# Four stacked graph layers on one core: inputs laid out transposed on the host, small chains merged, new PSUM homes and load order

## The reference

```python
# layer 0: Xp = x Wp + bp (8 heads of 32); out = relu(tanh(adj * (Xp C^T) Xp^T) Xp)
# layer 1: two hypergraph convolutions D^-1 H B^-1 H^T (x W^T) + b with H = (adj != 0);
#          between them relu and a LayerNorm with gamma and beta; result y + x
# layer 2: e = leaky_relu(s_j + s_i + ab), T = adj*exp(e) / row sum;
#          relu( x Wk0 + T x Wk1 + T T x Wk2 + biases )
# layer 3: xg = x * sigmoid(deg Wd + bd); qk = sigmoid(xg Wqk^T + bqk);
#          S = (qk qk^T) * adj / row sum; relu( S xg Wl^T + bl + xg Wr^T )
x = layernorm(x + L0(x, adj)); x = layernorm(x + L1(x, adj))
x = layernorm(x + L2(x, adj)); x = layernorm(x + L3(x, adj))
```

## Time and profile before

| | before |
|---|---|
| median of 3 runs | 2132.2 us (2131.32 to 2135.13) |
| span of the profiled execution | 2128.7 us |
| busy: PE, PE weight loads | 1964.9 us (92%), 1659.1 us (78%) |
| busy: VectorE, ScalarE, GpSimd | 1660.7 us (78%), 1271.3 us (60%), 862.6 us (41%) |
| DMA | 97.20 MB, 46 GB/s on average |
| share of the chain that ended last | PE 45%, DVE 25%, issue 14%, ACT 10%, POOL 5% |

### The profile page before, as it was taken

One profiled execution on the slowest core, in us unless ns is written; L12 is line 12 of the kernel. 1 busy time (PEld: TensorE's weight loads), 2 busy tenths in 40 slices (PEclk: granted clock), 3 DMA queues, 4 the chain that ended last, 5 costly groups with the idle time before them and its releaser, 6 DMA issues.

```text
span 2128.7 us, 52096 instructions
## 1 busy us (share of the span) xinstructions
PE 1964.9 (92%) x15270; PEld 1659.1 (78%) x15270; DVE 1660.7 (78%) x4520; ACT 1271.3 (60%) x2508; POOL 862.6 (41%) x1677
## 2 busy tenths in 40 slices
...
DMA packets 106517, 97.20 MB, mean 46 GB/s; under 512 B 12928, under 2 KB 97664, under 8 KB 106496
## 3 DMA queue, kind: packets, MB, share of 16 engines
...
...
## 4 chain that ended last, share of the span: by engine, by line
PE 45%; DVE 25%; issue 14%; ACT 10%; POOL 5%; DVEq 1%; SPq 0%; ACTq 0%; DMA 0%; POOLq 0%
PE psum L983 27%; DVE stats L669 5%; PE psum L1162 3%; PE psum L996 3%; PE psum L1105 3%; PE psum L1113 3%; ACT z L600 3%; PE psum L1034 2%; DVE res L882 2%; DVE hid L704 2%; DVE hid_stats L802 2%; POOL hid_rstd L422 2%; DVE xT_lo L662 2%; ACT hid_relu L507 2%; ACT e_neg L584 2%
## 5 line engine op out<-in xcount | busy, mean ns | idle before, releaser
L413 POOL TENSOR_TENSOR xg_lo<-xg,xg_hi 128x512 fp32r<-128x512 f32 x64 | 82.5, 1289 | 649.1 <-ACT xg_hi L463 649.1
L481 ACT ACTIVATE x<-res,shift,rstd 128x256 f32<-128x256 f32 x512 | 280.2, 600 | 13.6 <-POOL shift L395 12.2
L463 ACT ACTIVATE xT_hi<-psum 128x512 fp32r<-128x512 f32 x128 | 76.7, 599 | 306.7 <-PE psum L996 306.7
L669 DVE BATCH_NORM_STATS2 stats<-res 128x6 f32<-128x256 f32 x512 | 192.8, 419 | 8.9
L983 PE MATMUL psum<-wk_hi,xT_hi 128*128 128x258 f32 (+1 forms) x512 | 192.8, 377 | 1.1 <-DVE xT_lo L662 1.1
L388 POOL TENSOR_TENSOR var_eps<-mean_var,eps 128x2 f32<-128x2 f32 x256 | 50.6, 198 | 349.9 <-DVE mean_var L678 349.9
L392 POOL TENSOR_TENSOR rstd<-var_eps,minus_half 128x2 f32<-128x2 f32 x256 | 179.3, 700 | 20.0
L600 ACT ACTIVATE z<-hid_relu,hid_bias,hid_rstd 128x512 f32<-128x512 f32 x128 | 97.5, 809 | 137.9 <-POOL hid_bias L425 137.9
L983 PE MATMUL psum<-wk_hi,xT_lo 128*128 128x258 f32 (+1 forms) x512 | 174.2, 340 | 0.0
L983 PE MATMUL psum<-wk_lo,xT_hi 128*128 128x258 f32 (+1 forms) x512 | 173.8, 340 | 0.0
L689 DVE TENSOR_TENSOR masked<-psum,adjT 128x512 f32<-128x512 f32 x256 | 158.4, 682 | 6.9 <-PE psum L1013 6.9
...
## 6 DMA issues: line engine op xcount, KB each, us to landing
x_in<-in_x SPq DMA_DIRECT2D x64, 256.0 KB, 2.8
x<-x_in SPq DMA_DIRECT2D x64, 256.0 KB, 2.3
adjT<-adjT SPq DMA_DIRECT2D x128, 128.0 KB, 2.0
out<-x SPq DMA_DIRECT2D x64, 256.0 KB, 2.2
...
wk_f<-in_L_gnn_Wk SPq DMA_DIRECT2D x3, 256.0 KB, 6.1
```

Of the source, the lines that this page charges most:

```text
L413: pool.tensor_tensor(xg_lo[:, :, :, :], xg[:, :, :, :], value(xg_hi[:, :, :, :]), ALU.subtract) \
L463: return act.activation(dst, src, ACT.Copy).then_inc(sem(name), 1)
L481: last = act.activation(xs[k + 1][:, g, :], res[k][:, g, :], ACT.Identity, scale=rstd[k][:, g:g + 1], bias=shift[k][:, g:g + 1])
L669: last = dve.bn_stats(stats[k][:, g, :], res[k][:, g, :])
```

## The change

1. The host lays the inputs out: `xt` (x transposed) and `adj_t` (adj transposed) beside x, each weight group in one array (`w0` to `w3`) and each group of vectors in one (`v0` to `v3`). The transposes of x, adj and the weights on TensorE go, with their evictions. adj_t is loaded from HBM four times, once for each stage that needs it, in place of the copies inside SBUF; x is loaded to `x0` from HBM.
2. `xT0_hi` is made by ScalarE from SBUF, and `xT0_lo` by GpSimd as the first operation of its turn, in place of VectorE.
3. VectorE: the last column of `inc_b` by `tensor_tensor` (times one) in place of `tensor_copy`; sums and reciprocals of both graphs of `mix` and of `hop1` in one operation each; `node_r` without `deg_p`.
4. GpSimd: `qk + 1` by `tensor_scalar`; `x1_rest` in one add, as layer 1 is computed at half size (W2, beta and b2 halved, eps quartered).
5. Waits are put so that the one for this turn's data comes last. Every tenant has a new bank. SyncE's turn has a new order and a sixth stage, which holds only the store.
6. The weights' preparation is spread out: `prepare_0` ahead of turn 0, the others ahead of turns 0 to 3, engine by engine.

```diff
+    ("rz_0", 4, 4, "rz_read_0"), ("rz_1", 0, 4, "rz_read_1"), ("xp", 3, 0, "xp_read"),
+    ("mix_0", 5, 4, "mix_read_0"), ("xT2", 7, 2, "xT2_lo"), ("prop", 6, 1, "prop_read"), ("xpT", 2, 0, "xpT_read"),
+    ("mix_1", 4, 4, "mix_read_1"), ("deg", 0, 3, "gate"), ("y0_0", 3, 2, "y0_read_0"), ("y0_1", 7, 2, "y0_read_1"),
+    ("pxT", 5, 1, "pxT_lo"), ("xcT", 6, 0, "xcT_read"), ("y12_0", 2, 2, "y12_read_0"),
+    ("hid_0", 5, 1, "hid_read_0"), ("si", 0, 2, "e_both"), ("xT3", 4, 3, "xg"), ("hid_1", 1, 1, "hid_read_1"),
+    ("y12_1", 2, 2, "y12_read_1"), ("att_0", 0, 0, "masked_0"), ("att_1", 1, 0, "masked_1"),
+    ("att_2", 4, 0, "masked_2"), ("att_3", 7, 0, "masked_3"), ("hop1_0", 5, 2, "hop1_read_0"),
+    ("hop1_1", 6, 2, "hop1_read_1"), ("hop2", 6, 2, "hop2_read"), ("zT_0", 1, 1, "zT_lo_0"),
+    ("zT_1", 0, 1, "zT_lo_1"), ("qkT", 4, 3, "qk_tanh"), ("y1_0", 1, 1, "y1_read_0"), ("y1_1", 0, 1, "y1_read_1"),
+    ("headsT", 3, 0, "headsT_read"), ("gram", 2, 3, "scores"), ("conv", 1, 1, "res1"), ("heads", 5, 0, "res0"),
...
+                if on[1]:
+                    await_on_sp("masked_3", p[1])
+                    sp.dma_start(adjT[0][:, :, :].rearrange("p g n -> p (g n)"),
+                                 rows_at(adj_t, (t.i - 1) * (G * P * P))).then_inc(sem("adj0_loaded"), 16)
+                    await_on_sp("res0", p[1])
+                    sp.dma_start(xs[0][:, :, :], pair_at(x, (t.i - 1) * (G * P * D))).then_inc(sem("x0_loaded"), 16)
                 if on[4]:
-                    await_on_sp("x4", n[4])
-                    sp.dma_start(pair_at(out, (t.i - 4) * (G * P * D)), xs[4][:, :, :]).then_inc(sem("stored"), 16)
+                    await_on_sp("scores", p[4])
+                    await_on_sp("deg", p[4])
+                    sp.dma_start(adjT[3][:, :, :].rearrange("p g n -> p (g n)"),
+                                 rows_at(adj_t, (t.i - 4) * (G * P * P))).then_inc(sem("adj3_loaded"), 16)
+                if on[3]:
+                    await_on_sp("alpha", p[3])
+                    sp.dma_start(adjT[2][:, :, :].rearrange("p g n -> p (g n)"),
+                                 rows_at(adj_t, (t.i - 3) * (G * P * P))).then_inc(sem("adj2_loaded"), 16)
+                if on[5]:
+                    await_on_sp("x4", n[5])
+                    sp.dma_start(pair_at(out, (t.i - 5) * (G * P * D)), xs[4][:, :, :]).then_inc(sem("stored"), 16)
+                if on[0]:
+                    await_on_sp("xT0_hi", p[0])
+                    await_on_sp("xT0_lo", p[0])
+                    sp.dma_start(xt_in[:, :, :, :].rearrange("p c g n -> p (c g n)"),
+                                 rows_at(xt, t.i * (G * P * D))).then_inc(sem("xt_loaded"), 16)
+                    await_on_sp("inc", p[0])
+                    await_on_sp("edge_w", p[0])
+                    sp.dma_start(adjT[1][:, :, :].rearrange("p g n -> p (g n)"),
+                                 rows_at(adj_t, t.i * (G * P * P))).then_inc(sem("adj1_loaded"), 16)
+
+            def prepare_0():
+                sp.dma_start(wts0[:, :], w0).then_inc(sem("w_0"), 16)
+                sp.dma_start(vec0[:, :], v0.partition_broadcast(P)).then_inc(sem("w_0"), 16)
+
+            def prepare_1():
+                sp.dma_start(wts1[:, :], w1).then_inc(sem("w_1"), 16)
+                sp.dma_start(vec1[:, :], v1.partition_broadcast(P)).then_inc(sem("w_1"), 16)
+                sp.dma_start(wts2[:, :], w2).then_inc(sem("w_2"), 16)
+                sp.dma_start(vec2[:, :], v2.partition_broadcast(P)).then_inc(sem("w_2"), 16)
+                sp.dma_start(wts3[:, :], w3).then_inc(sem("w_3"), 16)
+                sp.dma_start(vec3[:, :], v3.partition_broadcast(P)).then_inc(sem("w_3"), 16)
+
+            turns(sp, turn, [(0, prepare_0), (1, prepare_1)])
...
+                if on[0]:
+                    wait(pool, "xp", p[0])
+                    wait(pool, "xT0_hi", n[0])
+                    pool.tensor_tensor(xT0_lo[:, :, :, :], xt_in[:, :, :, :], value(xT0_hi[:, :, :, :]), ALU.subtract) \
+                        .then_inc(sem("xT0_lo"), 1)
...
                     wait(pool, "x1", n[1])
-                    wait(pool, "res1", p[1])
-                    pool.tensor_tensor(x1_rest[:, :, :], xs[1][:, :, :], xs[1][:, :, :], ALU.add) \
-                        .then_inc(sem("x1_twice"), 1)
-                    wait(pool, "x1_twice", n[1])
-                    pool.tensor_tensor(x1_rest[:, :, :], x1_rest[:, :, :], rows(b2_bc), ALU.add) \
+                    pool.tensor_tensor(x1_rest[:, :, :], xs[1][:, :, :], rows(b2_half), ALU.add) \
                         .then_inc(sem("x1_rest"), 1)
                 if on[4]:
-                    rstd_of(3, t)
-                if on[3]:
-
+                    rstd_of(3, n[4], p[4])
+                if on[3]:
                     wait(pool, "qk_tanh", n[3])
-                    pool.tensor_tensor(qk[:, :, :, :].rearrange("p c g n -> p (c g) n"),
-                                       qk[:, :, :, :].rearrange("p c g n -> p (c g) n"),
-                                       ones[:, :].unsqueeze(1).to_broadcast([P, NC * G, P]), ALU.add) \
+                    pool.sem_inc(sem("pool_waits"), 1)
+                    pool.tensor_scalar(qk[:, :, :, :], qk[:, :, :, :], 1.0, 1.0, ALU.add, ALU.mult) \
                         .then_inc(sem("qk"), 1)
                 if on[2]:
-                    rstd_of(2, t)
-                if on[1]:
-                    rstd_of(1, t)
+                    rstd_of(2, n[2], p[2])
+                if on[1]:
+                    rstd_of(1, n[1], p[1])
...
-                    act.activation(adjT[0][:, :, :].rearrange("p g n -> p (g n)"), ps("adjT")[:, 0:G * P],
-                                   ACT.Copy).then_inc(sem("adjT_read"), 1)
+                    wait(act, "xt_loaded", n[0], 16)
+                    hi(xT0_hi[:, :, :, :], xt_in[:, :, :, :], "xT0_hi")
...
+            def prepare_0():
+                act.wait_ge(sem("w_0"), 32)
+                act.activation(wp_hi[:, :, :], wp_f[:, :, :], ACT.Copy).then_inc(sem("w_hi"), 1)
+
+            def prepare_1():
+                act.wait_ge(sem("w_1"), 32)
+                act.activation(w1_hi[:, :, :], w1_f[:, :, :], ACT.Copy).then_inc(sem("w_hi"), 1)
+                act.mul(b2_half[:, :], b2_bc[:, :], 0.5).then_inc(sem("b2_half"), 1)
+                act.mul(gamma_h[:, :], gamma_c[:, :], 0.5).then_inc(sem("halves_1"), 1)
+                act.wait_ge(sem("halves_1"), 1)
+                for k in range(NK):
+                    last = act.activation(w2_f[:, k, :], w2_raw[:, k, :], ACT.Copy, scale=gamma_h[:, k:k + 1])
+                last.then_inc(sem("w2_f"), 1)
+                act.wait_ge(sem("w2_f"), 1)
+                act.activation(w2_hi[:, :, :], w2_f[:, :, :], ACT.Copy).then_inc(sem("w_hi"), 1)
+
...
+            turns(act, turn, [(0, prepare_0), (0, prepare_1), (1, prepare_2), (1, prepare_3), (3, prepare_4)])
...
-                if on[0]:
-                    wait(dve, "xT0_hi", n[0])
-                    wait(dve, "xp", p[0])
-                    lo(xT0_lo[:, :, :, :].rearrange("p c g n -> p (c g n)"), ps("xT0"),
-                       value(xT0_hi[:, :, :, :]).rearrange("p c g n -> p (c g n)"), "xT0_lo")
...
+                    wait(dve, "mix_1", n[4])
+                    sums, _ = both("mix_0", "mix_1", slice(D, D + 1))
+                    dve.tensor_scalar(att_s[:, :].unsqueeze(2), sums, 1e-6, None, ALU.add).then_inc(sem("attn_0"), 1)
+                    wait(dve, "attn_0", n[4])
+                    dve.reciprocal(att_r[:, :], att_s[:, :]).then_inc(sem("attn_1"), 1)
+                    wait(dve, "res3", p[4])
+                    wait(dve, "r_bias", n[4])
+                    wait(dve, "attn_1", n[4])
+                    _, in_order = both("mix_0", "mix_1", slice(D, D + 1))
...
+                    dve.tensor_scalar(inc[:, :, :], adjT[1][:, :, :], 0.0, None, ALU.not_equal).then_inc(sem("inc"), 1)
+                    wait(dve, "prop", p[0])
+                    wait(dve, "adj1_loaded", n[0], 16)
+                    dve.tensor_tensor(inc_b[:, :, P:P + 1], adjT[1][:, :, 0:1], ones[:, 0:G].unsqueeze(2), ALU.mult) \
+                        .then_inc(sem("edge_w"), 1)
                     wait(dve, "inc", n[0])
...
+            def prepare_1():
+                dve.wait_ge(sem("w_1"), 32)
+                dve.wait_ge(sem("consts"), 1)
+                for k in range(NK):
+                    last = dve.tensor_scalar(beta_bc[:, k, :], ones[:, :], beta_c[:, k:k + 1], 0.5, ALU.mult, ALU.mult)
+                last.then_inc(sem("beta_bc"), 1)
+                dve.wait_ge(sem("w_hi"), 2)
+                lo(w1_lo[:, :, :], w1_f[:, :, :], value(w1_hi[:, :, :]), "w_lo")
+                dve.wait_ge(sem("w_hi"), 3)
+                lo(w2_lo[:, :, :], w2_f[:, :, :], value(w2_hi[:, :, :]), "w_lo")
+                dve.wait_ge(sem("beta_turned"), 1)
+                dve.tensor_copy(beta_w2[:, :], ps("conv")[:, 0:D]).then_inc(sem("beta_w2"), 1)
...
```

(19 more changed lines are left out.)

987 lines of the change are left out of this document (456 added, 531 removed), and 5 rows, old and new, of the table TENANTS.

## The result

| kernel | median us | runs | against the kernel before, 95% interval | profiled span us | mean granted clock |
|---|---|---|---|---|---|
| before, beside it | 2133.28 | 4 | 1 | 2128.7 | 0.986 |
| after | 2279.58 | 4 (2278.72 to 2284.47) | 1.0698 [1.0681, 1.0715] | 2276.9 | 0.952 |

The change makes the kernel 7.0% slower. The forecast was 2159 us with 2118 to 2200: the sign was right, the size was not, and the range does not hold the time.

The account below looks back on a forecast made before the run. A turn's period, on a chain through all engines, was taken as the bound: 1.51 - 0.5 - 0.45 = +0.56 us over 62 turns, +35, start -8, giving 2155.7; with 3.5 for the median 2159 us, range 2118 to 2200.

Parts of the forecast that it names:

- The mechanism: Turn's close: `xT0_lo` on GpSimd queues behind `rstd_of(1)`, so `xp` moves away from the variance of `res1` by +1.51 us.
- The variance to `xp`: From the end of `res1`'s variance to the start of `xp`: 2.82 us where it was 1.31, +1.51 us a turn.
- the last rival: TensorE before `xp`: idling about 2 us halves its clock for a while; no size of its own; chance 0.02.
- The term of the handovers: At `xT2_hi`, `xT2_lo` and `alpha`, putting the late wait last saves 0.45 us a turn, at most 0.46.
- What VectorE gives back: VectorE beside GpSimd's `qk`: a shorter hold lets the variance of `res1` come 0.5 us earlier, at most 0.74.
- the rival "not held": VectorE's new operation beside `qk` is not held: +0.32 us a turn, 2144 us; chance 0.22.
- One of the rivals' times: TensorE's removed work counts in full, 0.57 + 0.45 us a turn: 2065 us; chance within the 0.17.
- Start and end: Before and after the looped turns: spread-out preparation gains 8 us at the start, between 2 and 13; the end 0.
- Costed at nothing: SyncE's `xt` load behind the store, adj loads, new PSUM banks, `x1_rest` and `deg_p`: 0, banks at worst 0.1 us.

Follow-up runs that it names:

- the kernel with fillers: The kernel after, with fourteen products that nothing needs put on TensorE ahead of the wait for `xT0_lo`: 2206.23 us, 1.0352 of the kernel before.
- the mends: Kernel after with `xT0_lo` ahead of `rstd_of(1)`: 2107.57 us; also ahead of `rstd_of(2)`, `xt` load before store: 2091.28; five wait pairs restored: 2070.84; layer 3 adj load first: 2056.9.

## Why the prediction was right and wrong

- **The mechanism held.** `xT0_lo` behind `rstd_of(1)`, TensorE idle 1.5 to 2.5 us before `xp`, released by GpSimd, `res1` 0.1 to 0.4 behind `conv`: each is in the trace. The variance to `xp` was to take 2.82 us and takes 3.04: `var_eps` comes 0.07 later, by the order of its two waits, and 0.18 of issue stand ahead of `xT0_lo`, where I had put nothing.
- **The step that failed is the last rival.** "TensorE's longer idle stretch (about 2 us before `xp`) halves its clock for a while", chance 0.02, counted with the slow cases at no price of its own. It happens in 48 of 59 turns and costs 73 us, half of the loss. The evidence against it was one row, a `gram` behind 2.27 us of idling, and it couldn't bear that. The reading of the row was right: `gram` covers 1.16 us, in the kernel after the falls come 0.0 to 1.1 us behind the start of `xp`, and the clock stays up behind the row too. But one event says little where the clock spares every fifth or sixth turn: the kernel after keeps it in 11 of 59. Windows of the kernel before, behind that `gram`:

```profile
2096.00:2097.00 1.00, 1.00 (x10) 0.96 (x10) 0.06 (x1) 0.00 (x0) 0.84 (x2) 1.00 0.67 228
2097.00:2098.00 1.00, 1.00 (x6) 0.83 (x5) 0.37 (x1) 0.00 (x0) 0.06 (x1) 1.00 0.10 34
```

  A forecast that makes TensorE idle where it never did should have priced the half clock, from the work behind the stretch: some 3 us at half speed are 1.5 us a turn, 90 us over 60. That case gives 2249 us, and with a fair chance the range would have reached there.
- **The term of the handovers was mis-sized.** Forecast -0.45 us a turn; the trace has +0.21 from `xp` to `conv`. At the three places the gain is 0.23 us against the kernel before, half of what was taken: the gaps fell to 0.10 to 0.13 and not to 0.03 to 0.07. Five other handovers lost 0.33 us by the same rewriting, 0.26 of it between `xp` and `conv`. I had read their 0.03 to 0.07 us as "handovers with one late wait", and they were handovers with the late wait first and one behind it: I compared durations, not the order of the waits in the code. Some 0.2 us of the 0.44 isn't found in these. The relu and `e_exp` keep part of it (0.08 and 0.03 us with their order put back, 0.03 and 0 in the kernel before); the rest stays open.
- **What VectorE gives back** was 0.5 and is 0.65 at the start of `res1`, 0.69 by its variance. The argument was right in part: a two-input product is held, as I assumed, by `qk` for as long as it lasts. But in nearly every turn of the kernel after the product starts 0.05 us ahead of `qk` and takes 0.155 us; that it escapes is luck of the order. `qk` takes 0.62 us, near my lower bound of 0.58 and under the 0.8 that I took. So the rival "not held" described the turn, by a reason that is wrong.
- **The sum without the clock**: -0.69, +1.73 and +0.21 make +1.25 us a turn, where I had -0.5, +1.51 and -0.45, +0.56 in all. Over 62 turns that puts the forecast's sum at about 2202 us; the kernel with fillers measured 2206, just over the top of the range. Of the 121 us by which the forecast is short, 47 are what that kernel takes more than the forecast, most of it the handovers (0.66 us a turn, 41 us), and 73 are the clock. One of the rivals' times was added up wrongly: 0.57 + 0.45 a turn and the start's 8 give 2061 us and not 2065; nothing rests on it.
- **Start and end.** `xp` of the third pair starts at 81.84 us instead of 89.19: 7.4 us earlier, forecast 8. The first starts at 17.5 us (forecast 19 to 20). By the fifth pair the loss of the partly filled turns has taken 6.5 of it again.
- **Costed at nothing**: SyncE's load of `xt` was hidden in the kernel after, as said; without `xT0_lo` at the end of the line it isn't, and two of the mends are moves in SyncE's list. The PSUM banks show no wait of their own; they weren't tried apart.
